# Block product and inverse root for the head variance, and row norm on ScalarE, in a joined loop

## The reference, cut to what matters

```python
# L0_attn, per head of 32 values (16 heads)
mu = o.mean(-1, keepdims=True)
var = o.var(-1, keepdims=True)
o = (o - mu) * lax.rsqrt(var + EPS)
out = jax.nn.silu(g) * o @ Wout
x = x + out
# L0_ffn on layernorm(x): blocks of 32 features
scales = max(max(abs(block)) / 7.5, eps)
q = nearest_on_grid(block / scales)        # 6-bit float grid
x = x + (q * scales) @ wd.T + bias         # wd quantised likewise
```

## Time and profile before

| | |
|---|---|
| median of 3 runs (lowest, highest) | 1158.45 us (1156.43, 1624.27) |
| profiled execution: its time / its span | 1155.84 us / 1154.6 us |
| busy TensorE, VectorE, ScalarE, GpSimd | 1132.4, 749.6, 537.2, 244.3 us |
| mean granted clock of TensorE | 0.999 |

### The profile page before, as it was taken

The page is one execution under the profiler, slowest core; times in us unless marked ns, Lnnn a source line. Parts: engine busy times, 40 slices in busy tenths (PEclk is TensorE's granted clock), DMA queues, the critical chain, the costliest instruction groups (busy, mean ns, idle before and its releaser), DMA issues.

```text
span 1154.6 us, 21737 instructions
## 1 busy us (share of the span) xinstructions
PE 1132.4 (98%) x8721; PEld 845.5 (73%) x8721; DVE 749.6 (65%) x1524; ACT 537.2 (47%) x1037; POOL 244.3 (21%) x308
## 2 busy tenths in 40 slices
PE   7999999999999999999999999999999999999997
PEld 4665488776658777777777777777888778887886
DVE  6367478769894656666566666666797876546632
ACT  3244457653222655656565656565554532223421
POOL 2300013266740432121212122221432100000000
PEclk9999999999999999999999999999999999999999
DMA  9759710110205264444444444454810502224211
GB/s 351 273 212 404 278 55 1 40 44 1 110 19 183 40 137 100 92 92 93 92 93 93 92 92 99 91 101 79 112 19 1 83 5 33 37 37 76 34 37 37
DMA packets 325671, 111.57 MB, mean 97 GB/s; under 512 B 301834, under 2 KB 302908, under 8 KB 321348
## 3 DMA queue, kind: packets, MB, share of 16 engines
q1 hardware_dynamic: 324224, 109.11, 37.4%
q10 hardware_dynamic: 1348, 1.09, 0.4%
HBM read 65.59 MB, written 20.97 MB: 75 GB/s over the span
## 4 chain that ended last, share of the span: by engine, by line
PE 88%; DVE 6%; SPq 3%; DMA 1%; issue 1%; ACT 1%; POOL 0%; DVEq 0%; ACTq 0%
PE bank L303 64%; SPq L1871 3%; PE bank L1972 3%; PE bank L583 2%; PE bank L601 2%; PE bank L1988 2%; PE bank L1163 2%; PE bank L259 2%; PE bank L519 1%; PE bank L1185 1%; PE bank L1130 1%; PE bank L1127 1%; PE bank L1114 1%; PE bank L2445 1%; DVE xT L320 1%
## 5 line engine op out<-in xcount | busy, mean ns | idle before, releaser
L1909 POOL COPY PT<-W 32x512 f32<-32x512 f32 x120 | 83.8, 698 | 308.3 <-DVE W L2122 243.4
L2111 DVE CUSTOM_DVE_ANT_0 W<-bank,W 128x512 f32<-128x512 f32 x128 | 80.8, 687 | 101.8 <-PE bank L1972 98.2
L2202 ACT ACTIVATE K<-bank,vecT 128x512 f32<-128x512 f32 x64 | 43.8, 689 | 164.1 <-PE bank L303 164.1
L2223 ACT ACTIVATE W<-W,low 128x512 f32<-128x512 f32 x128 | 90.7, 711 | 16.9 <-DVE low L2111 16.9
L303 PE MATMUL bank<-xT,wT 128*128 128x512 f32 x384 | 92.6, 390 | 0.4 <-DVE wT L320 0.3
L303 PE MATMUL bank<-Wkv,Wq 128*128 128x512 f32 x384 | 92.7, 395 | 0.0
L303 PE MATMUL bank<-Wkv,ctxT 128*128 128x512 f32 x384 | 92.0, 394 | 0.0
L303 PE MATMUL bank<-ctxT,Wkv 128*128 128x512 f32 x384 | 90.1, 392 | 1.2 <-DVE ctxT L320 1.2
L303 PE MATMUL bank<-Wq,Wkv 128*128 128x512 f32 x384 | 89.8, 390 | 0.0
L303 PE MATMUL bank<-woT,hR 128*128 128x512 f32 x384 | 87.8, 390 | 0.6 <-DVE W_late L3081 0.5
L303 PEld LDWEIGHTS bank<-Wkv,ctxT 128*128 128x128 f32 x384 | 70.8, 188 | 22.2 <-ACT K L2202 5.7
(11 more groups left out here) (378 smaller groups left out, 2117.6 us busy)
## 6 DMA issues: line engine op xcount, KB each, us to landing
PT<-W SPq DMA_DIRECT2D x360, 64.0 KB, 2.1
W<-ctx_turned SPq DMA_DIRECT2D x16, 1024.0 KB, 5.9
W<-in_ctx_dram SPq DMA_DIRECT2D x8, 1024.0 KB, 10.6
ctx_turned<-ctxT SPq DMA_DIRECT2D x8, 1024.0 KB, 7.6
ctx_turned<-W SPq DMA_DIRECT2D x8, 1024.0 KB, 6.7
XT<-in_ctx_dram SPq DMA_DIRECT2D x4, 1024.0 KB, 11.6
XT<-in_L_ffn_wi_dram SPq DMA_DIRECT2D x64, 64.0 KB, 2.1
raw_own<-in_ctx_dram SPq DMA_DIRECT2D x3, 1024.0 KB, 11.0
```

The source lines that it names most:

```text
L1909: pool.tensor_copy(there, here).then_inc(kept_p.s, 1)
L2111: dve.tensor_tensor_reduce(out=PR[:, j, :], in0=bank[:, 4 + j % 4, :], in1=mask, scale=1.0, scalar=3.0e38, op0=ALU.add, op1=ALU.min, accum ...
L2202: act.activation(K[:, m, :], bank[:, n % 4, :], ACT.Identity, bias=pcol("L1_xattn_bk", m)).then_inc(ring_a.s, 1)
L2223: act.activation(PR[:, j, :], PR[:, j, :], ACT.Exp, bias=low[:, j:j + 1], scale=-1.0, accum_out=total[:, j:j + 1]).then_inc(expd.s, 1)
```

## The change

The variance is taken by one product with the whole `block` (128 x 128, 1/32 in blocks of 32), which leaves it repeated on all 32 partitions of its head. ScalarE takes the inverse root from PSUM to `root_at(g)` in one activation, for groups 0 and 1 by a copy first and the root later, in place (`early_root_a`). `variance_v`, `deviation_pool`, `widen_a` and `widen_pe` are gone. The quantiser's row norm moves to ScalarE (`normalise_rows_a`), for which the mean is negated on VectorE and multiplied on GpSimd. The orders of the queues change around it.

```diff
-            if l == 1 and g >= G // 2 or l == 5:
+            if l == 1 and g >= G // 2 or l in (2, 5):
                 p(ins)
                 ins = pool.tensor_tensor(shift[:, g:g + 1], shift[:, g:g + 1], rstd[:, g:g + 1], ALU.mult)
...
-                    deviation_pool(t - 1)
...
             def bias_pool(g):
...
-                pool.wait_ge(normed.s, normed(nth("normed", 2, g)))
+                pool.wait_ge(normed_a.s, normed_a(G // 2 + g))
...
             def mean_of_pe(g):
                 pe.wait_ge(low_o.s, low_o(g))
                 if g:
-                    pe.wait_ge(var_v.s, var_v(g - 1))
+                    pe.wait_ge(var_a.s, var_a(g - 1))
...
             def variance_pe(g):
                 pe.wait_ge(sqr.s, sqr(g))
-                for t in range(C):
-                    ins = pe.matmul(bank[:, 5, 4 * t:4 * t + 4], sq_at(g)[:, t * P:(t + 1) * P], block[:, 0:P:GDV], start=True, stop=True)
-                ins.then_inc(var_pe.s, 1)
+                pe.matmul(bank[:, 5, :], block[:], sq_at(g), start=True, stop=True).then_inc(var_pe.s, 1)
...
             def turn_blocks_pe(g):
                 pe.wait_ge(scaled.s, scaled(g))
-                if g + 2 < G:
-                    pe.wait_ge(ynm.s, ynm(g + 2))
...
                 for t in range(G + 3):
                     if t == 1:
                         gate_pe(5)
-                    if t == 3:
-                        pe.wait_ge(sg_v.s, sg_v(1))
-                        widen_pe(0)
                     if 1 <= t <= G:
                         attend_pe(t - 1)
-                    if 4 <= t < G + 3:
-                        widen_pe(t - 3)
                     if t < G:
                         scores_pe(t)
...
+                    if t == 3:
+                        pe.wait_ge(sg_v.s, sg_v(2))
+                    if 3 <= t < 6:
+                        project_pe(t - 3, range(1))
                     if 1 <= t < 6:
                         mean_of_pe(t - 1)
...
-                    if t == 3:
-                        pe.wait_ge(sg_v.s, sg_v(2))
                     if 3 <= t:
-                        project_pe(t - 3)
+                        project_pe(t - 3, range(1, C) if t < 6 else range(C))
...
             def normal_v(g):
-                dve.wait_ge(wide_pe.s, wide_pe(g))
+                if g < 2:
+                    dve.wait_ge(root_a.s, root_a(g))
+                else:
+                    dve.wait_ge(var_a.s, var_a(g))
                 dve.wait_ge(gated.s, gated(g))
-                dve.tensor_tensor(y[:, g % 3, :], y[:, g % 3, :], bank[:, 6, :], ALU.mult).then_inc(ynm.s, 1)
+                dve.tensor_tensor(y[:, g % 3, :], y[:, g % 3, :], root_at(g), ALU.mult).then_inc(ynm.s, 1)
...
-                row_stats_v(g)
+                row_stats_v(g, negated=l == 1)
...
-                normalise(xq, 2, g)
-                dve.wait_ge(normed.s, normed(nth("normed", 2, g)))
+                dve.wait_ge(normed_a.s, normed_a(G // 2 + g))
...
                 for t in range(G):
                     if t:
                         low_of_v(t - 1)
-                    if 3 <= t:
-                        normal_v(t - 3)
                     for r in range(4):
                         masked_v(t, r)
+                    if 3 <= t:
+                        normal_v(t - 2)
...
                         key_weights_v(0)
                     if t < 3:
                         gate_last_v(5 + t)
+                    if t == 2:
+                        normal_v(0)
...
-                    if 1 <= t:
-                        variance_v(t - 1)
...
                 low_of_v(7)
-                normal_v(5)
+                normal_v(6)
                 quantise_v(4)
-                variance_v(7)
                 for g in (5, 6, 7):
                     add_v(g)
-                    if g < 7:
-                        normal_v(g + 1)
+                    if g == 5:
+                        normal_v(7)
...
+            def variance_a(g):
+                act.wait_ge(var_pe.s, var_pe(g))
+                if g < 2:
+                    act.copy(root_at(g), bank[:, 5, :]).then_inc(var_a.s, 1)
+                else:
+                    act.wait_ge(ynm.s, ynm(g - 1))
+                    act.activation(root_at(g), bank[:, 5, :], ACT.Abs_reciprocal_sqrt, bias=eps[:]).then_inc(var_a.s, 1)
+
+            def early_root_a(g):
+                act.wait_ge(var_a.s, var_a(g))
+                act.activation(root_at(g), root_at(g), ACT.Abs_reciprocal_sqrt, bias=eps[:]).then_inc(root_a.s, 1)
+
+            def normalise_rows_a(g):
+                act.wait_ge(rstd_ok.s, rstd_ok(nth("rstd", 2, g)))
+                act.activation(xq[:, g, :], X[:, g, :], ACT.Identity, scale=rstd[:, g:g + 1],
+                               bias=shift[:, g:g + 1]).then_inc(normed_a.s, 1)
...
                 for t in range(1, G + 5):
                     if t <= G:
                         attended_a(t - 1)
-                    if t + 1 < G:
-                        sigmoid_a(t + 1)
-                    if 2 <= t < G + 2:
-                        widen_a(t - 2)
+                    if t == 1:
+                        sigmoid_a(2)
+                    elif t == 2:
+                        sigmoid_a(6)
+                        sigmoid_a(7)
                     if t <= G:
                         square_a(t - 1)
                     if t <= 2:
                         gate_out_a(5 + t)
+                    if t == 1:
+                        for g in (3, 4, 5):
+                            sigmoid_a(g)
+                    elif t == 2:
+                        early_root_a(0)
+                    if 4 <= t < G + 4:
+                        normalise_rows_a(t - 4)
                     if t >= 5:
                         blocks_a(t - 5)
-                    if t <= C:
-                        key_weights_a(t - 1)
+                    if 3 <= t <= 5:
+                        key_weights_a(t - 2)
+                    if t <= G:
+                        variance_a(t - 1)
+                    if t == 2:
+                        early_root_a(1)
+                        key_weights_a(0)
```

More of the change, by code:

```diff
@@ L223, in nth @@
         def nth(kind, l, g):
-            return side_by_side.get((kind, l, g), l * G + g) - (G // 2 if kind == "normed" and l >= 2 else 0)
+            return side_by_side.get((kind, l, g), l * G + g) - (kind == "normed") * (G // 2 * (l >= 2) + G * (l >= 3))
         def row_stats_v(g, negated=False):
@@ L936, in l0_gated_attention @@
             w = sb(ph, "w2", [P, G, GH])
-            var = sb(ph, "var", [P, 2, GH])
-            half = sb(ph, "mhalf", [P, GH])
+            eps = sb(ph, "eps", [P, 1])
             def xb(h, c, lo, n):
@@ L961, in l0_gated_attention @@
                 for kind, l, g in (("xsum", 2, t - 6), ("xsum", 1, t - 3), ("stats", 2, t - 3), ("stats", 3, t - 6),
-                                   ("rstd", 3, t - 7), ("rstd", 2, t - 3), ("normed", 2, t - 4 if t < 10 else t - 3 if t == 10 else G),
-                                   ("normed", 2, 6 if t == 9 else G), ("normed", 3, t - 7)):
+                                   ("rstd", 3, t - 7), ("rstd", 2, t - 3), ("normed", 3, t - 7)):
                     if kind == "xsum" and t >= 8:
@@ L966, in l0_gated_attention @@
                     if 0 <= g < G:
-                        first = G if kind == "xsum" else 2 * G
+                        first = {"xsum": G, "normed": 3 * G}.get(kind, 2 * G)
                         side_by_side[kind, l, g] = first + sum(k[0] == kind for k in side_by_side)
@@ L978, in l0_gated_attention @@
             sq_at = lambda g: W[:, 0, 3, :] if g < 2 else sq[:]
-            wide_at = lambda g: y[:, 2, :] if g < 1 else wide[:]
+            root_at = lambda g: y[:, 2, :] if g < 1 else wide[:]
             by_group = lambda ap: ap.rearrange("f (c g r) -> f (c g) r", c=2, g=G)
@@ L1003, in l0_gated_attention @@
             var_pe = signal("b_var_pe")
[L1004 to L1007, removed]
+            var_a = signal("b_var_a")
+            root_a = signal("b_root_a")
             gated = signal("b_gated")
@@ L1029, in gpsimd @@
                     row_stats_pool(1, g)
-                p(pool.memset(half[:], -0.5))
+                p(pool.memset(eps[:], EPS))
                 p(pool.memset(augw[:], 0.0))
@@ L1089, in gated_pool @@
                                    ALU.mult).then_inc(gated.s, 1)
-            def deviation_pool(g):
-                pool.wait_ge(var_v.s, var_v(g))
-                pool.tensor_tensor(var[:, g % 2, :], var[:, g % 2, :], half[:], ALU.pow).then_inc(rst.s, 1)
             def scale_pool(g):
@@ L1143, in variance_pe, with project_pe @@
                 pe.wait_ge(sqr.s, sqr(g))
-                for t in range(C):
-                    ins = pe.matmul(bank[:, 5, 4 * t:4 * t + 4], sq_at(g)[:, t * P:(t + 1) * P], block[:, 0:P:GDV], start=True, stop=True)
-                ins.then_inc(var_pe.s, 1)
[L1148 to L1164, removed]
```

(23 more changed lines are left out.)

5 lines of the change are left out of this document (removed).

## The result

The changed kernel takes 1162.57 us (median of 6 runs, 1161.05 to 1163.42), the kernel before 1156.8 us (median of its now 6 runs). The ratio is 1.0047, with a 95% interval of 1.0036 to 1.0059: 0.5% slower, which is small but clear of the scatter. The profiled execution took 1162.36 us. The forecast had been 1.2 us more; it is 5.8.

What follows compares the result with a forecast made beforehand. TensorE (98% busy) bounds the loop, then the chain of the last quantised groups. TensorE's saving repays the t=3 stall, the tail adds 1.2: 1158.45 + 1.2 = 1159.6 us, own range 1158 to 1161, full range 1155.2 to 1163.3.

Steps and rivals of the forecast that it cites:

- the likeliest case: Whole kernel: stall at t=3 paid back by t=8, longer tail costs +1.2 us, 1159.6 us in all; chance 0.5.
- signs that the forecast had set for being right: One table load near 250.2, TensorE idle some 3 us, iterations 0.37 to 0.57 shorter, late reduces, last block transposes 1 us late.
- TensorE's work: Loop: transposes removed -3.6 us, larger variance products +0.6, means covered by the first projection chunk -0.6; -3.6 us at most.
- The stall at t=3: TensorE waits before the first projection chunk for group 0's normalisation, behind ScalarE's queue: 3.05 us idle, bounds 1.8 to 3.3.
- The bound of the root: ScalarE's inverse root, absent from the trace: between 0.63 us (plain sigmoid) and 0.82 (row normalisation), taken as 0.69.
- The drain: 1380 ns beside the table load at t=2, by the page: 1.35 us more at t=3, so 1161.0; chance 0.02.
- The clock: Slower rival: TensorE's clock falls in the 3 us stall, 1.7 us at 256.5, so 1161.3; chance 0.07.
- The saving pays it back: Iterations t=4 to 7 regain the 2.1 us lost at t=3: 0.25 behind after t=7, 0.2 ahead when projection 5 ends.
- The tail: Last quantised groups: chain over GpSimd and ScalarE moves group 6's reduce +0.3 and group 7 +1.2 us; bounds 0.4 to 1.7.
- The gain of TensorE's saving: Faster rival: TensorE's 3.6 us comes through with stall and tail hidden but for some tenths, 1155.2 us; chance 0.2.
- Tables loaded twice an iteration: Slower rival: Square and root in different ScalarE tables, deciding at t=8 alone, 1161 to 1162.3 us; chance 0.07.
- A shared table: Half-gain rival: sigmoid and root share a table, no load at t=2, stall 1.8 us, about 1158.4; chance 0.12.

Runs made afterwards that it cites:

- e7: Changed kernel with ScalarE's key-weight casts early and the quantiser's row normalisation back on VectorE, leaving only the variance part: 1156.68 us, ratio to before 0.9999.
- e1: Changed kernel with ScalarE's two key-weight casts issued before the square of t=2 instead of behind both early roots: 1158.11 us, ratio to before 1.0016.
- e5: Changed kernel with the row normalisation back on VectorE and the casts left late, so the stall of t=3 stays: 1160.84 us, ratio to before 1.0034.
- e11: Changed kernel, loop untouched, with 84 transposes of 32x32 at the start of TensorE's queue (17776 instructions): 1160.45 us, ratio to before 1.0031.
- e2: Changed kernel with three extra unused fp32 products of 512 columns inside the stall of t=3: 1158.94 us, ratio to before 1.0023.
- e3: Changed kernel with ScalarE's row normalisation ahead of the square in each step instead of behind it: 1160.57 us, ratio to before 1.0037.
- e6: Changed kernel with both the casts early and the row normalisation ahead of the square: 1157.79 us, ratio to before 1.0014.
- e8: The kernel of e1 with 84 extra transposes of 32x32 at the start of TensorE's queue (17776 instructions): 1155.58 us, ratio to before 0.9993.
- e9: Kernel before with 43 extra transposes of 32x32 at the start of TensorE's queue (17863 instructions): 1159.36 us, ratio to before 1.0021.
- e12: The kernel of e7 with 84 extra transposes of 32x32 at the start of TensorE's queue (17776 instructions): 1154.13 us, ratio to before 0.9976.

## Why the prediction was right and where it fell short

The time lies in the range (1155.2 to 1163.3) and the sign is right, but the likeliest case said +1.2 us and its own range 1158 to 1161; measured are +5.8. That the range holds is in part luck. It was built on 1158.45 us, the median of three runs of which one took 1624.27; six runs give 1156.8. The range's upper end lies 4.9 us above the first number, and from the second the same sum would have ended at 1161.7, below the 1162.57 measured. Two of the signs that the forecast had set for being right failed (TensorE's iterations shorter up to the last, the block transposes about 1 us late), and one for being wrong came true, a clock below 1.00. The loop's account by the runs is: the variance part alone -2.7 us (e7 against before), the wait at t=3 +2.9, the clock +1.6, the rows on ScalarE +1.6, together +3.5 (the four must add up to this, as e7, e1 and the changed kernel are steps of one ladder; e5 gives 1.6 for the rows once more, beside the stall); and behind the loop 2.1 (e11) to 3.0 us (the profile).

- **TensorE's work.** "-3.6 us, the most that TensorE can give". It holds as a bound: e7, with stall and rows gone, gives 2.7. One block product takes 0.86 us in the chain, as forecast; the iterations of t=4 to 6 became shorter by 0.46, 0.48 and 0.36 (forecast 0.57, 0.57 and 0.37).
- **The stall at t=3.** Right in cause and size: 3.05 us forecast, 3.26 measured, and the chain step by step. The bound of the root was good too, 0.72 and 0.69 for the 0.69 taken. The drain that the Trainium skill (ScalarE: Activation LUTs, What ACT_TABLE_LOAD costs) adds to a table load did not appear: behind the load of 1.28 us at 250.08 the root starts at 251.38.
- **The clock.** Priced at 1.7 us, measured 1.64 (e2), and given a chance of 0.07. This is the first step that failed: the sum put the clock at nothing. The forecast held against it that the clock was 1.00 in both stretches; but in those stretches TensorE had never been idle for as long, as the forecast itself says, so the rows said nothing against it. The one row that spoke, spoke for it. It should have stood beside the stall with even chances, and the likeliest time would have been near 1161.
- **"The saving pays it back" until t=8.** It did at t=4 to 6, 0.5, 0.5 and 0.4 us. At t=7 it turned round by 0.6: VectorE's maximum of group 2 waited 1.59 us for rows that stand behind the square, VectorE had no idle from there on and was late with the next addition of the linear layer (L1396, over at 300.65), and TensorE idled 0.90 us for it. The 0.66 us before the maximum of group 3 come behind that idle. The forecast had seen this order for group 4 alone ("ScalarE's rows stand behind the square of group 7") and not asked it of groups 2 and 3, where means too come only after a linear product. Moving the rows ahead gives 0.7 to 0.8 us (e3, e6).
- **The tail.** The mechanism is right: the reduce of group 7 is late, released by ScalarE. Relative to the loop before it, the tail cost 1.0 us (2.4 us behind when t=9 begins at 315.89 for 313.46, 3.4 at the last block transposes); forecast were 1.4. For group 6 the forecast had moved the reduce by 0.3; it moved by 2.69 (327.90 for 325.21), as the whole loop was late by then. The rows on ScalarE cost 1.6 us in all, 0.8 of it by their order (e6 against e1) and 0.9 by their chain (e7 against e6).
- **Behind the loop.** No step and no rival had a word of it. The change leaves that code as it was, and the forecast took it for a shift. It costs 2 to 3 us, more than the likeliest case's whole sum, and by e8, e9 and e11 it is the place of the code.
- **The rivals.** The gain of TensorE's saving is what e12 shows, 1154.13, once stall, rows and the place of the code are out of the way. Tables loaded twice an iteration: fell, the loop has one load more than before (at 250.08, beside the sigmoid's at 232.04), and Square runs beside the root. A shared table: fell as well.

## What to carry to other kernels

When an engine's only cover is its queue, write down for each instruction that moves what stands behind it on its engine and who waits for that: this gave the 3.3 us stall to 0.2 us, and the same question asked once more of every iteration would have shown the 0.8 us of the rows. A stall of several us on a TensorE that had none should be priced with the fall of its clock, here half as much again. And a change that removes instructions moves all later code: for effects below 0.5%, compare with the instruction count padded to the old one before a part of the change is blamed. And three runs with one far outlier are too few for a base: here its median was 1.65 us too high, more than the forecast change.

## What the runs showed of the hardware

- Two passes of 512 fp32 columns took 2.05 us instead of 1.05 to 1.10 after 3.26 us of idle, at a granted clock of 0.51; the clock was 1.00 again 4 us after. With 0.49 us of idle at the same place (e2) it stayed at 1.00. The Trainium skill (TensorE: Matmul & The Clock Gate, What's actually happening) has the fall on idleness, and the trace agrees.
- The clock fell in every profile that has the 3.26 us stall (changed, e3, e5, e11), and not always at its end. In e5 TensorE resumes at 257.68 at a clock of 1.00 and the fall comes after that; its stretches of 2 us:

```profile
258.00:260.00 2.00, 2.00 (x6) 0.93 (x5) 2.00 (x5) 0.64 (x2) 0.00 (x0) 0.75 0.00 0
260.00:262.00 2.00, 2.00 (x4) 0.97 (x3) 2.00 (x3) 1.47 (x3) 1.27 (x1) 0.50 0.00 0
```

- 43 transposes in otherwise idle time, at the very start of TensorE's queue, made a kernel 3.0 us slower (1156.4 to 1159.4), and 84 made another one 2.5 us faster (1158.1 to 1155.6), through waits of 0.2 to 1.4 us in bursts of 128 short products. The products that wait are the same to one in two kernels whose queues differ by 255 instructions, nearly one 16.4 KB transfer, and move by six where the code moves by 12 instructions (e2). 39 of 40 such waits end 1.25 to 1.57 us after the end of an instruction transfer. TensorE waits for its own code there; the view of waits names no releaser, and what fills the time behind the transfer is open.
- ScalarE's inverse root with a vector as bias takes 0.72 us from SBUF and 0.69 from PSUM for 512 columns, its row normalisation with two vectors 0.81.
